# First gates and routing spread over the first heads, blanks sent one group later, attention outputs turned behind the weighing

## What is computed

```python
def _L0_attn_ref(x, W_w, W_b, proj_w, proj_b, ln_g, ln_b, rpb):
    ...  # 16 heads of 8, q, k, v from one projection
    attn = jnp.einsum('bhqd,bhkd->bhqk', q, k) / jnp.sqrt(jnp.float32(d))
    attn = jnp.where(causal[None, None], -jnp.inf, attn)
    attn = attn + bias[None]
    w = jax.nn.softmax(attn, axis=-1)
    o = jnp.einsum('bhqk,bhkd->bhqd', w, v)
    ...
    out = o @ proj_w.T + proj_b
    y = x + out
    ...  # layer norm of y with ln_g, ln_b
def _L0_ffn_ref(x, gate_W, gate_b, W1, b1, W2, b2):
    logits = jnp.einsum('btd,de->bte', x, gate_W) + gate_b
    top1 = jnp.argmax(logits, axis=-1).reshape(-1)
    ...  # each of the 4096 tokens goes through its one of 8 experts
```

## Time and profile before

| | before |
|---|---|
| median of 3 runs (lowest, highest) | 759.73 us (759.12, 760.5) |
| profiled execution, its own time | 761.72 us |
| span of that execution | 759.6 us |
| mean granted clock of TensorE | 0.915 |
| PE busy | 627.2 us (83%) |
| DVE busy | 450.1 us (59%) |
| ACT busy | 372.5 us (49%) |
| POOL busy | 469.5 us (62%) |

### The profile page before, as it was taken

How to read it: one execution, slowest core, us unless ns; L and a number is a source line. 1 busy time by engine, 2 the same in 40 slices (tenths; PEclk the granted TensorE clock), 3 DMA queues, 4 the chain that set the end, 5 groups by cost and what they waited for, 6 DMA issues and landing times. The chain is left out here.

```text
span 759.6 us, 15493 instructions
## 1 busy us (share of the span) xinstructions
PE 627.2 (83%) x4794; PEld 520.9 (69%) x4794; DVE 450.1 (59%) x1825; ACT 372.5 (49%) x904; POOL 469.5 (62%) x591
## 2 busy tenths in 40 slices
PE   5967888989898888989999259698996799999830
PEld 4755666666666666668999248587996699999720
DVE  6296677777677776745444375544764133333696
ACT  6535666667576666763444264322454233333331
POOL 7355577877778677835555483265777266666434
PEclk9759999999999999999999756999999799999965
DMA  8443444454444345226788310061111377774443
GB/s 256 144 133 146 162 136 147 127 141 148 134 123 126 123 126 190 95 56 191 229 244 242 103 54 1 1 210 40 56 51 56 113 234 240 242 232 139 125 125 111
DMA packets 85888, 105.42 MB, mean 139 GB/s; under 512 B 9584, under 2 KB 66160, under 8 KB 85808
## 3 DMA queue, kind: packets, MB, share of 16 engines
q1 hardware_dynamic: 75168, 77.84, 34.9%
q0 software_dynamic: 7616, 17.32, 6.7%
q10 hardware_dynamic: 3024, 9.29, 3.3%
HBM read 69.43 MB, written 34.98 MB: 137 GB/s over the span
## 5 line engine op out<-in xcount | busy, mean ns | idle before, releaser
L1422 POOL DMA_INDIRECT tok<-h_y_out,h_x_in x78 | 74.7, 957 | 48.5 <-DVE h_y_out L1728 36.3
L917 DVE CUSTOM_DVE_ANT_0 a_high<-a_p_s,f_shared 128x256 f32<-128x256 f32 x168 | 69.9, 416 | 42.2 <-PE a_p_s L585 41.1
L1415 POOL DMA_INDIRECT slots<-k_xn,k_pos x64 | 63.8, 997 | 38.6 <-issue 13.7
L1176 POOL TENSOR_TENSOR a_high<-a_high,a_top 128x768 f32<-128x768 f32 x42 | 61.5, 1464 | 32.2 <-DVE a_top L917 32.0
L825 ACT ACTIVATE a_prob_more<-a_p_t 128x384 f32<-128x384 f32 x128 | 61.7, 499 | 37.7 <-PE a_p_t L599 29.4
L584 PE MATMUL a_p_s<-a_kst,a_qst 72*128 72x256 bf16 x256 | 73.5, 289 | 5.4 <-DVE a_top L917 5.3
L1721 DVE TENSOR_TENSOR h_hid<-h_k,h_pre 128x512 f32<-128x512 f32 x39 | 27.0, 691 | 83.9 <-ACT h_pre L1633 83.9
L1505 PE MATMUL h_k<-h_x_t,h_w 128*128 128x256 f32 x312 | 76.0, 388 | 0.0
L1222 POOL DMA_INDIRECT tok<-a_fill,a_e_ids x46 | 44.3, 963 | 43.2 <-DVE a_fill L1103 34.1
L597 PE MATMUL a_p_t<-k_ident,a_low 128*128 128x128 f32 x168 | 49.8, 297 | 15.9 <-ACT f_w_sh L825 11.2
L1505 PEld LDWEIGHTS h_k<-h_x_t,h_w 128*128 128x128 f32 x312 | 57.8, 195 | 6.5
(11 more groups left out here) (273 smaller groups left out, 1902.9 us busy)
## 6 DMA issues: line engine op xcount, KB each, us to landing
h_w<-in_W SPq DMA_DIRECT2D x39, 384.0 KB, 3.3
a_e_w<-in_W SPq DMA_DIRECT2D x23, 514.0 KB
a_kst<-parts SPq DMA_DIRECT2D x32, 288.0 KB
a_qst<-parts SPq DMA_DIRECT2D x32, 288.0 KB
slots<-a_fill ACTq DMA_DIRECT2D x21, 432.0 KB, 4.2
parts<-a_part SPq DMA_DIRECT2D x32, 192.0 KB, 2.4
h_x_in<-slots SPq DMA_DIRECT2D x39, 144.0 KB, 3.2
h_top<-tok SPq DMA_DIRECT2D x16, 256.0 KB, 3.5
```

What stands on the lines that cost most here:

```text
L917: dve.tensor_tensor_reduce(out=out[:, x, :], in0=p_s[n % banks][:, cols], in1=bias_q[:, h, at], scale=1.0, scalar=-3.0e38, op0=ALU.add, op ...
L1176: pool.tensor_tensor(arg[:, 0:subtracted, :], arg[:, 0:subtracted, :], top[r][:, t, 0:subtracted].unsqueeze(2).to_broadcast([P, subtracted ...
L1415: pool.indirect_dma_start(D["slots1"], bass.IndirectOffsetOnAxis(ap=R.pos[n][:, t:t + 1], axis=0), R.xn[:, t, :], None).then_inc(done, 16)
L1422: pool.indirect_dma_start(D["tok1"], bass.IndirectOffsetOnAxis(ap=x_in[r][:, k, P:P + 1].bitcast(I32), axis=0), y_out[r][:, k, :], None).t ...
```

## The change

PE: no gates in the setup. The gates of stages 0 to 2 stand behind the heads of group 0, those of 3 to 5 behind group 1, of 6 and 7 behind group 2. `rank` stands behind the first head of group 4. `turn_o` moves from before `weigh` to behind it. DVE: maxima of groups 0 and 1 follow one another; routing is 16 steps, from the first head of group 3 on, step 4 being empty while PE ranks. The two steps that read the ranks signal `counted`, for which the first `turn_o` waits. ACT: `exponent` of group 0 comes before the first part of batch 2, its second part moves into the loop; the send of the blanks of group n stands behind the fourth head of group n+1. POOL: scatters begin in group 12, not 10, and end in group 61 as before.

```diff
+GATED = {0: (0, 1, 2), 1: (3, 4, 5), 2: (6, 7)}
+RANKED = 4
+SCATTER0 = 12
...
         def turn_o(pe, b):
             pe.wait_ge(s["o_raw_ok"], b + 1)
             wait_if(pe, s["s_ok"], 2 * b)
+            if b == 0:
+                pe.wait_ge(s["counted"], 2)
...
             values(pe, 0)
-            gate(pe, 0)
             for g in range(2, NG):
                 turn_x(pe, g)
-                gate(pe, g - 1)
                 if g == 4:
                     project(pe, 1)
-            gate(pe, NG - 1)
+            project_bv(pe)
+            pe.wait_ge(s["xt_ok"], NG)
             for x in range(QUAD):
                 score(pe, 0, x)
             project(pe, 2)
-            project_bv(pe)
             for x in range(QUAD):
                 score(pe, 1, x)
-            rank(pe)
             for n in range(last):
                 b, g = divmod(n, quads)
                 for x in range(QUAD):
                     if n + 2 < last:
                         score(pe, n + 2, x)
                     turn(pe, n, x)
+                    if n == RANKED and x == 0:
+                        rank(pe)
+                for part in GATED.get(n, ()):
+                    gate(pe, part)
...
-                if g == 1 and b:
-                    turn_o(pe, b - 1)
                 if g == 2 and b:
                     turn_on(pe, b - 1)
                 if g == 3 and b:
                     project_o(pe, b - 1)
                 if n:
                     weigh(pe, n - 1)
+                if g == 1 and b:
+                    turn_o(pe, b - 1)
...
+            exponent(act, 0)
             first_part(act, 2)
-            second_part(act, 2)
-            exponent(act, 0)
...
-                    if x == 3 and fill_of(n) is not None:
-                        send_fill(act, fill_of(n))
+                    if x == 3 and n and fill_of(n - 1) is not None:
+                        send_fill(act, fill_of(n - 1))
...
-                    if x == 1 and g == 0 and 3 <= b + 2 < B:
+                    if x == 1 and g == 0 and b + 2 < B:
                         second_part(act, b + 2)
...
             shift_x(dve, NG - 1)
+            widen_bv(dve)
             third_part(dve, 1)
-            for x in range(QUAD):
-                row_max(dve, 0, x)
-            widen_bv(dve)
-            read_logits(dve)
-            route_pick(dve)
+            add_bv(dve)
+            for m in range(2):
+                for x in range(QUAD):
+                    row_max(dve, m, x)
             rest(dve, 2, (0, 1))
-            route_mask(dve)
-            third_part(dve, 2)
-            add_bv(dve)
-            for x in range(QUAD):
-                row_max(dve, 1, x)
...
-                    route_step(dve, QUAD * n + x)
+                    route_step(dve, QUAD * (n - min(GATED) - 3) + x)
...
-                if n == FILLS0 + 2:
+                if n == SCATTER0:
                     for u in range(2):
                         pool.wait_ge(fill_sent[u], 16 * len(range(u, FILLS0, 2)))
                     pool.wait_ge(s["routed"], 1)
-                at, steps = n - FILLS0 - 2, last - 4 - FILLS0
+                at, steps = n - SCATTER0, last - 2 - SCATTER0
```

More of the change, by code:

```diff
@@ L415, in first_half @@
             "xn_ok", "x_turned", "xt_ok", "gated", "w_ok", "bv_wide_ok", "bv_projected", "b_proj_ok", "residual_ok",
[L416 removed]
+            "route", "mask_ok", "ranked", "counted", "routed", "owned", "fill_zero",
             "e_turned", "e_ids_ok", "e_x_ok", "e_up_ok", "e_pre_ok", "e_hid_ok", "e_down_ok", "e_y_ok", "fill_ok", "neg_ok", "biased",
@@ L998, in read_logits, with route_best, route_hits, route_pick @@
                                         R.gb[:].unsqueeze(1).to_broadcast(per_tile), ALU.add))
-        def route_pick(dve):
+        def route_best(dve):
             dve.wait_ge(s["tables"], 4)
             step(dve, dve.tensor_reduce(best[:], R.logits[:], X, ALU.max))
+        def route_hits(dve):
             step(dve, dve.tensor_tensor(hit[:], R.logits[:], best[:].unsqueeze(2).to_broadcast(per_tile), ALU.is_equal))
             step(dve, dve.tensor_tensor(hit[:], hit[:], em8, ALU.mult))
+        def route_pick(dve):
             step(dve, dve.tensor_reduce(first[:], hit[:], X, ALU.min))
@@ L1012, in route_count @@
             dve.wait_ge(s["ranked"], 1)
-            step(dve, dve.tensor_copy(count[:].rearrange("p e t -> p (e t)"), p_misc[:, E * NT:2 * E * NT]))
+            dve.tensor_copy(count[:].rearrange("p e t -> p (e t)"), p_misc[:, E * NT:2 * E * NT]).then_inc(s["counted"], 1)
+            dve.wait_ge(s["counted"], 1)
         def route_sum(dve):
@@ L1019, in route_rank, with route_offset @@
         def route_rank(dve):
-            step(dve, dve.tensor_tensor(slot[:], p_misc[:, 0:E * NT].rearrange("p (e t) -> p e t", e=E), upto[:], ALU.add))
+            dve.tensor_tensor(slot[:], p_misc[:, 0:E * NT].rearrange("p (e t) -> p e t", e=E), upto[:], ALU.add
+                              ).then_inc(s["counted"], 1)
+            dve.wait_ge(s["counted"], 2)
+        def route_offset(dve):
             step(dve, dve.tensor_tensor(slot[:], slot[:], count[:], ALU.subtract))
@@ L1056, in route_step @@
             if n == 0:
+                read_logits(dve)
+                route_best(dve)
+            elif n == 1:
+                route_hits(dve)
+            elif n == 2:
+                route_pick(dve)
+            elif n == 3:
+                route_mask(dve)
+            elif n == 5:
                 route_count(dve)
-            elif n == 1:
+            elif n == 6:
                 route_sum(dve)
-            elif n == 2:
+            elif n == 7:
                 route_rank(dve)
-            elif n == 3:
+            elif n == 8:
+                route_offset(dve)
+            elif n == 9:
                 route_totals(dve)
-            elif n == 4:
+            elif n == 10:
                 route_tiles(dve)
-            elif n == 5:
+            elif n == 11:
                 route_starts(dve)
-            elif n == 6:
+            elif n == 12:
                 route_slots(dve)
-            elif n == 7:
+            elif n == 13:
                 route_pos(dve)
-            elif n == 8:
+            elif n == 14:
                 route_owner(dve)
-            elif n == 9:
+            elif n == 15:
                 route_expert(dve)
@@ L1155, in _ @@
                         rest(dve, b + 3, (x - 2,))
-                    if (g, x) == (0, 3) and 3 <= b + 2 < B:
+                    if (g, x) == (0, 3) and b + 2 < B:
                         third_part(dve, b + 2)
```

## The result

| | before | after |
|---|---|---|
| median (lowest, highest), side by side on one chip, 4 runs each | 760.12 us (759.12, 766.08) | 730.2 us (729.06, 733.41) |
| profiled execution, its own time | 761.72 us | 729.18 us |
| span of that execution | 759.6 us | 726.7 us |
| mean granted clock of TensorE | 0.915 | 0.910 |
| PE busy | 627.2 us | 624.5 us |

The ratio is 0.9581, 95% interval 0.954 to 0.9621. The change makes the kernel about 30 us faster; the forecast was 738.7 us, 21 us faster than the median of 759.73. The direction held, the size did not.

A forecast was written before the change was run, and what follows sets the result against it. PE was the busiest engine up to 335 us, its waits deciding, with DVE the bound at 40 to 60 us. Terms -9.7 - 12.6 - 1.0 + 2.3 = -21.0 gave 740.7 us profiled, median 738.7, range 734 to 744.

The forecast's parts named there:

- step 4: Groups 0 to 6: gates return on PE, routing on DVE; group 7 starts at 84.1 us, +2.3 us.
- Step 1: Loop: outputs turned behind the weighing, so PE's waits for DVE at the turning fall under it; -9.7 us.
- the last wait: The turning wait at 323.64 us, 0.69 us; no gain was credited, as scatter and expert-row load come behind it.
- Step 2: Loop: blanks sent one group later, so ACT no longer holds PE at the third head; -12.6 us.
- The -1.0 us for groups 7 and 8: Groups 7 and 8: two PE waits for ACT, of the 6.5 us, go as well; -1.0 us.
- Steps 3 and 4: Setup without gates starts the loop at 33.5 us; then gates and routing in groups 0 to 6 put group 7 at 84.1.
- The +2.3 us: Groups 0 to 6: group 7 starts at 84.1 us against 81.78 before, with DVE the bound of groups 3 to 6.
- POOL's rival: Loop: the wait moves to POOL in seven batches with a scatter before the subtraction; price 7.4 us, 746.1 us, chance 0.12.
- the third rival: Loop: added transposes in a row make the clock fall once more per batch, 24 us; 762.5 us, chance 0.04.
- the first rival: Groups 0 to 2: PE's clock is at the upper level, 8.5 us less; 730.2 us, chance 0.2.
- The rule of the Trainium skill: Groups 0 to 2: throttled is the default clock, so PE stays at the lower level without setup gates; 5.5 us worse.

The follow-up runs named there:

- e1: The changed kernel with the outputs turned before the weighing again, blanks still sent a group later: 741.02 us, ratio 0.9731 to the kernel before.
- e2: The changed kernel with the blanks sent in the same group again, outputs still turned behind the weighing: 765.92 us, ratio 1.0036 to the kernel before.
- e6: The kernel before with only the two loop edits (blanks a group later, outputs turned behind the weighing): 727.14 us, ratio 0.9535.
- e8: The changed kernel with ranks counted behind the fourth head of group 4 and routing steps from the fifth on three heads later: 733.38 us, ratio 0.9618.
- e3: The changed kernel with both loop edits undone, leaving the setup, gates, ranking and routing changes: 763.88 us, ratio 1.0009 to the kernel before.
- e0: The changed kernel as it is, run a second time beside other early parts: 730.67 us, ratio 0.9553 to the kernel before.
- e11: The changed kernel with all gates in the setup, routing from the first head of group 0 and ranks counted in group 1: 728.39 us, ratio 0.9517.
- e12: The changed kernel with all gates in the setup and routing thinned to about every second head, groups 1 to 9: 722.56 us, ratio 0.9476.

## Why the prediction was too small

The mechanisms of steps 1 and 2 were right and their sizes too small; step 4 was priced too dear at group 7; and the clock falls that go with a long wait stood in no term. The sums, for the profiled executions: the forecast takes 21.0 us off the span, the trace 32.9.

| stretch | forecast | measured |
|---|---|---|
| to group 7 (81.78 before) | +2.3 | -2.5 |
| group 7 to the turning of group 9 (11.7 before; the -1.0 and the wait at this turning) | -1.8 | +0.7 |
| 13 periods between turnings | -21.5 | -28.8 |
| behind | 0 | -2.3 |

In the medians the miss is 8.5 us and not 11.9. The profiled execution of before lies 2.0 us above its median, which I carried over, and that of the change 1.0 below its own.

**Step 1, outputs turned: -9.7 forecast.** Mechanism right, and the undone edit cost some 11 us (e1). The 0.05 us that I left in each place isn't there, and the last wait (0.7 us), for which I gave nothing, went too: PE does not wait longer behind it, as the 1.39 us for the experts' rows are gone as well. The step took its gain for independent, which it is not: it holds only together with step 2 (e2). With both edits in the change, the sum was not hurt by that.

**Step 2, blanks a group later: -12.6 forecast in the loop.** Mechanism right, size too small: the 0.2 us a batch that I left for the copy of the values isn't there (109.17 stands without a bracket above). And I left out that these waits carry falls of the clock. Of the 7.3 us that the 13 periods gave beyond the forecast, 0.6 and 2.6 us are what I had left in the two steps, 0.7 is the last wait, and about 3.3 are two falls of the clock of 1.6 to 1.7 us that the trace of before has (200 to 210 us, and the earlier trace rows). I had priced one at 1.7 us, counted two, and used them only for the rival that it gets worse.

**The -1.0 us for groups 7 and 8 was mis-sized.** I took two of the eight waits of the earlier trace rows's third line for waits behind the send. In e6, where the routing stays as before, group 7 comes 3.4 us sooner (81.78 to 78.39) and the turning of group 9 4.3 us sooner (93.48 to 89.19). PE's waits for ACT in 30 to 94 us, before and then in e6:

```profile
PE a_p_t L597 <- ACT a_prob_more L825: 6.2, 6, 2.7
PE a_p_t L597 <- ACT f_w_sh L825: 1.1, 1, 1.1
```

```profile
PE a_p_s L584 <- ACT a_prob_more L825: 0.6, 1, 0.6
PE a_p_t L597 <- ACT a_prob_more L825: 0.2, 1, 0.2
```

The 7.3 us have become 0.8, and 1.6 us of that went over to waits for DVE's maxima. In the change little of it is left between group 7 and the turning of group 9, as DVE is the bound there (12.30 of 12.40 us):

```profile
79.32:91.72 12.40, 10.65 (x121) 7.58 (x117) 12.30 (x69) 8.76 (x22) 8.63 (x14) 1.00 0.46 162
```

**Steps 3 and 4, setup and groups 0 to 6.** They forecast a loop start at 33.5 and group 7 at 84.1; they came at 32.7 and 79.3. The starts of the loop, of the gates and of groups 3 and 7 on PE:

```profile
32.72 0.37 PE L587 MATMUL a_p_s<-a_kst,a_qst 72*128 72x256 bf16 x1
...
36.39 2.74 PE L542 MATMUL a_p_misc<-k_gate_w,k_xt 128*128 128x8 f32 x24
...
42.21 5.13 PE L542 MATMUL a_p_misc<-k_gate_w,k_xt 128*128 128x8 f32 x24
...
53.46 1.85 PE L542 MATMUL a_p_misc<-k_gate_w,k_xt 128*128 128x8 f32 x16
...
56.99 0.28 PE L587 MATMUL a_p_s<-a_kst,a_qst 72*128 72x256 bf16 x1
...
79.32 0.28 PE L587 MATMUL a_p_s<-a_kst,a_qst 72*128 72x256 bf16 x1
```

Groups 0 to 2 took 24.3 us (26.9 forecast), groups 3 to 6 took 22.3 (23.7), so that group 7 was put 4.8 us too late: 0.8 in the setup, 2.6 in groups 0 to 2, where I had chosen a value between the two clock levels, 1.4 in the routing. DVE as the bound of groups 3 to 6 was right (e8), and so was the ranking as no cost of its own. What the part costs depends on what stands beside it. Alone (e3) it brings group 7 at 77.6, 4.2 us sooner than before, and ends level. Beside the two other edits it puts group 7 at 79.3 and 79.7 (the change, twice) where e6 without it has 78.4, and the medians' ratios differ by 1.4 to 3.5 us to its cost, within overlapping intervals. The +2.3 us are near this second figure, but I had worked them out against the kernel before as it is, and there the trace says -2.5.

**By sums:** the loop edits alone are worth 0.0465 of the time, 35 us (e6), where I forecast 23.3; the early part takes a few of these back; 30 us remain.

**The rivals.** POOL's rival did not come: in the changed trace no period between turnings from group 9 on is over 15.71 us, with a scatter in front of the subtraction or not. The clock did not fall there: its granted clock is 1.00 in every 5 us from 80 to 350 us, although the loop turns as much as the third rival feared (I called the transposes over half of PE's instructions; they are 12 of the 28 of a plain group, and 16 with the turning). The number of the first rival (730.2) is the result, but by luck and not by its mechanism: it wanted the upper level in groups 0 to 2, and the changed trace has 0.50 from 40 to 50 us, gates at 5.13 us for 24 passes there and 2.74 and 1.85 (for 24 and 16) at mostly the upper level. The rule of the Trainium skill that I weighed (TensorE: Matmul & The Clock Gate, Part 1) would have made it 5.5 us worse; these rows show both levels in turn, and the groups took 24.3 us.

## What to carry to other kernels

When two waits of one engine stand in a row and the second hangs on a chain that the first does not move, removing the first alone gives nothing: find the one whose releaser is independent, and remove that first. Before spreading work over a stage, add up for each engine what it does while the other waits for it: here 9.7 us of gates kept DVE idle and DVE's routing then kept PE waiting, and putting all or half of the gates back into the setup was worth 8 us in the median. A new wait that leads the list may mark only where two engines meet; e8 moved it and gained nothing.

## What the runs showed of the hardware

**From 90 us on, each fall of the clock starts right behind a long wait.** The first row is from PE's timeline in e2, the other two are stretches of it, the granted clock being the third number from the end:

```profile
169.54 0.30 PE L600 MATMUL a_p_t<-k_ident,a_low 128*128 128x128 f32 x1 [2.52 <-ACT f_w_sh L831]
```

```profile
165.00:170.00 5.00, 2.43 (x28) 2.01 (x21) 3.17 (x19) 2.00 (x7) 4.55 (x6) 1.00 0.45 139
170.00:175.00 5.00, 4.96 (x37) 3.11 (x36) 0.99 (x5) 1.78 (x6) 3.50 (x5) 0.66 0.65 229
```

From 90 us to the end of the loop, the three traces with the sends in their own group throughout (before, e2, e3) have two, four and four such stretches, each right behind a wait for ACT of 1.6 us or of 2.5 us. The eleven with the sends moved in the loop have none, e1 with its 14 waits of up to 0.9 us included. Not every wait of 1.6 or 2.5 us is followed by a fall, and up to 90 us it is not so plain: in e1 and in the second run of the change (e0) the granted clock falls to 0.50 at about 82 and 84 us, where no wait is over 0.95 us but several stand close together. In the first run of the change it is 0.50 from 65 to 70 us, right behind the wait of 3.9 us at the ranking. So a long wait is what preceded the falls of the loop; that it is needed for one isn't shown. It fits that e2, with four, is 35 us slower than the change and not the 27 us of its waits.

**A DVE instruction with two operands in SBUF takes longer beside POOL.** The same product takes 0.43 us with POOL idle (at 43.94 in e11) and 1.57 us beside a POOL instruction that began 0.3 us earlier. DVE, and then POOL, in e12:

```profile
45.85 1.57 DVE L1013 TENSOR_TENSOR a_hit<-a_hit,k_expert_m 128x256 f32<-128x256 f32 x1
```

```profile
45.56 1.58 POOL L1198 TENSOR_TENSOR f_cos_sin<-f_cos_sin,a_top 128x768 f32<-128x768 f32 x1 [1.24 <-DVE a_top L924]
```

POOL's instruction ends at 47.14 and DVE's at 47.42, 0.28 us behind it, as if it had done its work after it. The Trainium skill (SBUF — State Buffer, section "SBUF: two separate sides") says that a DVE instruction with two SBUF inputs and a GpSimd instruction that reads SBUF take the shared port pair in turns, the later one blocked whole; these rows agree. My price of 12.4 us for the routing was read from instructions of which some were stretched so: in the trace of before two such instructions of 128x256 take 1.46 and 1.68 us (48.91 and 54.97), each beginning 0.3 us behind one of POOL's.
